# Adjacency counts in turns of sixteen parts, with one-hots of eight parts written side by side

## The reference

```python
# layer 0: mean over incoming edges
messages = h[src] @ W + b
out = segment_sum(messages, dst, N) / clip(deg, 1, None)[:, None]
# layer 3: h = relu(x @ W_in.T + b_in), then three times
out = segment_sum(norm * (h @ W.T)[row], col, N) + b
h = h + relu(out)
```

## Time and profile before

| | |
|---|---|
| median of 3 runs | 9669.24 us |
| profiled execution | 9702.59 us, span 9700.8 us |
| counting stage in it | 883 to 1957 us |
| TensorE, VectorE, ScalarE busy, whole span | 6251.8 (64%), 4831.9 (50%), 1756.7 us (18%) |
| mean granted clock of TensorE | 0.685 of 2.4 GHz |

### The profile page before, as it was taken

How to read it: one execution, slowest core, us unless ns; L and a number is a source line. 1 busy time by engine, 2 the same in 40 slices (tenths; PEclk the granted TensorE clock), 3 DMA queues, 4 the chain that set the end, 5 groups by cost and what they waited for, 6 DMA issues and landing times. The chain is left out here.

```text
span 9700.8 us, 148103 instructions
## 1 busy us (share of the span) xinstructions
PE 6251.8 (64%) x29798; PEld 4311.0 (44%) x29800; DVE 4831.9 (50%) x20045; ACT 1756.7 (18%) x3492; POOL 3219.5 (33%) x3353
## 2 busy tenths in 40 slices
PE   1512666677555455554555548777888888769999
PEld 1511333366333333333333325555555555568777
DVE  6887999932555555555555543333333333342222
ACT  0002666600111111111111111111111111110000
POOL 0103000000544444444444425555555555500000
PEclk9955555589666666666666665666666665669999
DMA  1051222254322222222222312222222222226666
GB/s 34 1 180 44 74 75 75 75 191 183 64 59 58 58 60 58 58 58 58 59 57 58 59 28 34 34 35 34 34 35 34 34 34 34 34 75 261 245 242 236
DMA packets 1052830, 765.90 MB, mean 79 GB/s; under 512 B 869013, under 2 KB 978277, under 8 KB 1033206
## 3 DMA queue, kind: packets, MB, share of 16 engines
q1 hardware_dynamic: 897158, 511.13, 18.3%
q0 software_dynamic: 131808, 243.11, 10.7%
q10 hardware_dynamic: 23776, 10.58, 0.4%
HBM read 659.36 MB, written 143.22 MB: 83 GB/s over the span
## 5 line engine op out<-in xcount | busy, mean ns | idle before, releaser
L1745 POOL DMA_INDIRECT rows<-node_rows_wide,idx_ring x1612 | 1533.9, 952 | 1649.4 <-DMA idx_ring<-sorted_pairs 1167.5
L1745 POOL DMA_INDIRECT rows<-node_rows,idx_ring x1612 | 1524.7, 946 | 1232.9 <-DMA idx_ring<-src_all 697.0
L1794 PE MATMUL ps_sum<-hots,act_ring 128*97 128x128 f32 x3224 | 742.1, 403 | 1536.5 <-DVE hots L1779 1184.2
L1794 PEld LDWEIGHTS ps_sum<-hots,act_ring 128*97 128x97 f32 x3224 | 612.6, 255 | 1908.2 <-DVE accT L1788 1448.8
L1782 DVE TENSOR_SCALAR hots<-iota,lane_all 128x128 f32<-128x128 f32 x1612 | 461.7, 287 | 1838.8 <-remote 1324.1
L1794 PE MATMUL ps_sum<-hots,msg 128*96 128x128 f32 x3224 | 724.2, 399 | 472.9 <-DVE hots L1782 239.2
L1821 PE MATMUL ps_e<-w1e,aT 128*128 128x384 f32 x1612 | 983.6, 757 | 25.1 <-DVE aT L1856 20.2
L1321 PE MATMUL ps_conv<-conv_rows,adj_ring 128*128 128x288 bf16 x7497 | 939.0, 287 | 47.3 <-DMA adj_ring<-adjacency 24.8
L1099 PE MATMUL ps_blocks<-dst_hot,src_hot 128*128 128x256 bf16 x2792 | 659.5, 416 | 410.6 <-ACT ps_blocks L1120 287.9
L1788 DVE TENSOR_TENSOR accT<-accT,ps_sum 97x128 f32 (+1 forms) x3224 | 907.1, 281 | 5.4 <-PE ps_sum L1794 4.0
L1794 PEld LDWEIGHTS ps_sum<-hots,msg 128*96 128x96 f32 x3224 | 624.9, 258 | 503.3 <-DVE accT L1788 411.7
(11 more groups left out here) (323 smaller groups left out, 6544.8 us busy)
## 6 DMA issues: line engine op xcount, KB each, us to landing
adj_ring<-adjacency SPq DMA_DIRECT2D x144, 2176.0 KB, 7.8
adjacency<-panels SPq DMA_DIRECT2D x588, 128.0 KB, 1.7
idx_ring<-sorted_pairs SPq DMA_DIRECT2D x1612, 1.0 KB
attr_ring<-sorted_attr SPq DMA_DIRECT2D x1612, 16.0 KB
rows<-node_rows_wide,idx_ring POOLq DMA_INDIRECT x1612
attr_ring<-sorted_attr SPq DMA_DIRECT2D x1612, 8.5 KB
rows<-node_rows,idx_ring POOLq DMA_INDIRECT x1612
sorted_attr<-in_edge_attr SPq DMA_DIRECT2D x5, 5000.0 KB
```

The lines of the kernel that those rows point to most:

```text
L1745: g.indirect_dma_start(out=rows[:, r, j, 0:width], out_offset=None, in_=table, in_offset=bass.IndirectOffsetOnAxis(ap=idx, axis=0)).then_i ...
L1794: last = pe.matmul(ps_sum[0:M, r % 2, j, :], what(r, j), hots[:, r % 2, j, :], start=True, stop=True)
```

## The change

- `GK` is 16, `HB` 2 and `BANKS` 8: a turn has sixteen parts, two turns are buffered, all eight banks are used, in plain rotation over all 637 panels. There are 175 turns, 2800 parts. The table entry of a part becomes its panel's number plus 1, and the bank is that number modulo 8.
- VectorE waits for the banks. For each half turn of eight parts (`HK`) it reads the table entry of the half's last part, waits for the matmuls that used the buffer, and waits on `emptied`. TensorE no longer reads or waits for that; it does one column load of 16 values a turn.
- The one-hots of eight parts come from one instruction each: `iota_h` now repeats each number eight times, the lanes of eight parts are read as a row of eight that repeats, and a TENSOR_TENSOR compare writes 128 x 8 and 256 x 8 values. Element (column, part) stands at 8 x column + part. So the matmul's operands, `src_hot[:, r, j // HK, :, j % HK]` and the same of `dst_hot`, have a step of eight bf16, 16 bytes, from column to column.
- ScalarE reads a block's 13 panel ends in one load, and its loop over blocks is written out for eight blocks, as the bank of a panel now depends on the block. A semaphore `passed_a` is counted up beside its wait.

```diff
--- before.py
+++ after.py
@@ -75,16 +75,17 @@
 BUCKETS = NB * NW
 NB_BITS = 64
 BASE = 0x20000000
-GK = 8
+GK = 16
+HALF = GK // 2
 LOG_P = 7
 PARTS = E // P + BUCKETS
 Q2 = -(-PARTS // GK)
 T2 = Q2 * GK
-HB = 4
+HB = 2
+HK = 8
 NK = -(-NW // 2)
 PANELS = NB * NK
-PANEL_BANK = tuple(k if k < 7 else k - 7 for k in range(NK))
-BANKS = 7
+BANKS = 8
 TT = -(-(T2 + 64) // P) * P
 KC = -(-T2 // (4 * P)) * 4
 TP = KC * P
@@ -97,7 +98,7 @@
 CB = SB // NC
 PANEL_COLS = tuple(min(2 * WD, NP - 2 * k * WD) for k in range(NK))
 assert CB * NC == SB and PANEL_COLS[NK - 1] == P
-assert TP <= 2 * SN and NK <= 13 and KEYS > E + P and NW <= 1 << WB and COLS % OCN == 0
+assert (NB - 1) % BANKS == 0 and TP <= 2 * SN and NK <= 13 and KEYS > E + P and NW <= 1 << WB and COLS % OCN == 0
 ZR = 8
 
 GB = 7
@@ -262,6 +263,7 @@
         gather_go = sem("gather_go")
         passed_t = sem("passed_t")
         passed_v = sem("passed_v")
+        passed_a = sem("passed_a")
         gathered = [sem(f"gathered{k}") for k in range(GPI)]
         src_kept = sem("src_kept")
         fields = sem("fields")
@@ -667,7 +669,7 @@
             part_to = accT[0:1, 0:2 * T2].bitcast(I32).rearrange("p (c t) -> p c t", c=2)
             panel_end = accT[64:65, 0:PANELS].bitcast(I32)
             lanes = tmp("lanes", [P, 2, TP], BF16)
-            iota_h = tmp("iota_h", [P, WD], BF16)
+            iota_h = tmp("iota_h", [P, WD, HK], BF16)
 
             with ExitStack() as ctx:
                 def stmp(name, shape, dt=F32):
@@ -709,7 +711,7 @@
                 put_at = stmp("put_at", [NB, NW + 1], I32)
                 info = stmp("info", [NB, NW + 1, 3])
                 panel_i = stmp("panel_i", [NB, 2, NW], I32)
-                panel_f = stmp("panel_f", [NB, 2, NW])
+                panel_f = stmp("panel_f", [NB, 1, NW])
                 end_i = stmp("end_i", [NB, NK], I32)
                 ps_t = ctx.enter_context(nc.psum_tensor("ps_keys", [P, 4, 512], F32))
                 ps_c = ctx.enter_context(nc.psum_tensor("ps_counts", [P, 512], F32))
@@ -720,7 +722,7 @@
                 @block.gpsimd
                 def _(g):
                     g.iota(lane_no[:, :], [[0, 1]], base=0, channel_multiplier=1).then_inc(made.sem, 1)
-                    g.iota(iota_h[:, :], [[1, WD]], base=0, channel_multiplier=0,
+                    g.iota(iota_h[:, :, :], [[1, WD], [0, HK]], base=0, channel_multiplier=0,
                            allow_small_or_imprecise_dtypes=True).then_inc(made.sem, 1)
                     g.memset(ones2[:, :], 1.0).then_inc(made.sem, 1)
                     g.memset(before2[:, :], 1.0).then_inc(made.sem, 1)
@@ -823,7 +825,7 @@
                     v.tensor_copy(end_i[:, NW // 2:NK], til_end[:, NW - 1:NW]).then_inc(ends_out.sem, 1)
                     step(v, v.memset(info[:, NW, 0:1], 1.0))
                     step(v, v.memset(info[:, NW, 1:2], float(NB << WB)))
-                    step(v, v.memset(info[:, NW, 2:3], float((PANELS + 2) << 12)))
+                    step(v, v.memset(info[:, NW, 2:3], float((PANELS + 1 << 12) + PANELS % BANKS * 2 * WD)))
                     link(v, v.tensor_scalar(row_no[:, 1:2], row_no[:, 0:1], float(1 << WB), None, ALU.mult))
                     step(v, v.tensor_scalar(info[:, 0:NW, 0], cnt[:, :], 1.0, None, ALU.add))
                     step(v, v.tensor_scalar(info[:, 0:NW, 1], iota[0:NB, 0:NW], row_no[:, 1:2], None, ALU.add))
@@ -838,18 +840,16 @@
                     of_window, panel = panel_i[:, 0, :], panel_i[:, 1, :]
                     link(v, v.tensor_copy(of_window, iota[0:NB, 0:NW]))
                     link(v, v.tensor_scalar(panel, of_window, 1, None, ALU.logical_shift_right))
-                    step(v, v.tensor_scalar(of_window, of_window, 1, 8, ALU.bitwise_and, ALU.logical_shift_left))
-                    link(v, v.tensor_copy(panel_f[:, 1, :], panel))
-                    step(v, v.tensor_copy(panel_f[:, 0, :], of_window))
-                    link(v, v.tensor_scalar(row_no[:, 1:2], row_no[:, 0:1], float(NK), 2.0, ALU.mult, ALU.add))
-                    link(v, v.tensor_scalar(til[:, :], panel_f[:, 1, :], row_no[:, 1:2], None, ALU.add))
-                    link(v, v.scalar_tensor_tensor(out=panel_f[:, 0, :], in0=panel_f[:, 1, :], scalar=512.0,
-                                                   in1=panel_f[:, 0, :], op0=ALU.mult, op1=ALU.add))
-                    link(v, v.tensor_scalar(panel_f[:, 1, :], panel_f[:, 1, :], float(BANKS), -512.0 * BANKS,
-                                            ALU.is_ge, ALU.mult))
-                    link(v, v.tensor_tensor(panel_f[:, 0, :], panel_f[:, 0, :], panel_f[:, 1, :], ALU.add))
-                    link(v, v.scalar_tensor_tensor(out=info[:, 0:NW, 2], in0=til[:, :], scalar=4096.0,
-                                                   in1=panel_f[:, 0, :], op0=ALU.mult, op1=ALU.add))
+                    step(v, v.tensor_scalar(of_window, of_window, 1, LOG_P + 1, ALU.bitwise_and, ALU.logical_shift_left))
+                    link(v, v.tensor_copy(til[:, :], panel))
+                    link(v, v.tensor_scalar(row_no[:, 1:2], row_no[:, 0:1], float(NK), None, ALU.mult))
+                    link(v, v.tensor_scalar(til[:, :], til[:, :], row_no[:, 1:2], None, ALU.add))
+                    link(v, v.tensor_copy(panel, til[:, :]))
+                    link(v, v.tensor_scalar(panel, panel, BANKS - 1, LOG_P + 2, ALU.bitwise_and, ALU.logical_shift_left))
+                    link(v, v.tensor_tensor(panel, panel, of_window, ALU.bitwise_or))
+                    link(v, v.tensor_copy(panel_f[:, 0, :], panel))
+                    link(v, v.tensor_scalar(til[:, :], til[:, :], 1.0, 4096.0, ALU.add, ALU.mult))
+                    link(v, v.tensor_tensor(info[:, 0:NW, 2], til[:, :], panel_f[:, 0, :], ALU.add))
 
                 def describe_tiles(v):
 
@@ -1049,8 +1049,8 @@
             with ExitStack() as ctx:
                 def btmp(name, shape, dt=F32):
                     return sbuf(name, shape, dt, ctx)
-                src_hot = btmp("src_hot", [P, HB, GK, P], BF16)
-                dst_hot = btmp("dst_hot", [P, HB, GK, WD], BF16)
+                src_hot = btmp("src_hot", [P, HB, GK // HK, P, HK], BF16)
+                dst_hot = btmp("dst_hot", [P, HB, GK // HK, WD, HK], BF16)
                 panels = btmp("panels", [P, NK, 2 * WD], F16)
                 target = btmp("target", [P, 2 * WD])
                 heavy_cell = btmp("heavy_cell", [P, NK, HV, 2 * WD], F16)
@@ -1067,15 +1067,19 @@
                     v.memset(no_lanes[:, :], 0.0).then_inc(nothing.sem, 1)
 
                     def hots(q, turn, r):
-                        past(v, block_mm, (q - (HB - 1)) * GK)
-                        v.sem_inc(passed_v.sem, 1)
-                        for j in range(GK):
-                            v.tensor_scalar(src_hot[:, r, j, :], iota_h[:, 0:P], lanes[:, 0, dyn(q * GK + j, 1)], None,
-                                            ALU.is_equal)
-                            last = v.tensor_scalar(dst_hot[:, r, j, :], iota_h[:, :], lanes[:, 1, dyn(q * GK + j, 1)], None,
-                                                   ALU.is_equal)
-                            if j % 4 == 3:
-                                last.then_inc(ends_hot.sem, 1)
+
+                        for n in range(GK // HK):
+                            if n * HK % HALF == 0:
+                                empty = v.value_load(part_to[0:1, 1, dyn(q * GK + n * HK + HALF - 1, 1)], min_val=1,
+                                                     max_val=PANELS + 1)
+                                past(v, block_mm, (q - HB) * GK + n * HK + HALF)
+                                v.sem_inc(passed_v.sem, 1)
+                                v.wait_ge(emptied.sem, empty)
+                            lane = [lanes[:, k, dyn(q * GK + n * HK, HK)].unsqueeze(1) for k in range(2)]
+                            v.tensor_tensor(src_hot[:, r, n, :, :], iota_h[:, 0:P, :],
+                                            lane[0].to_broadcast([P, P, HK]), ALU.is_equal)
+                            v.tensor_tensor(dst_hot[:, r, n, :, :], iota_h[:, :, :],
+                                            lane[1].to_broadcast([P, WD, HK]), ALU.is_equal).then_inc(ends_hot.sem, 1)
                     turns(v, [(hots, 0)], Q2, HB)
 
                 @block.tensor
@@ -1087,16 +1091,14 @@
 
                     def count(q, turn, r):
 
-                        panels_out = pe.value_load(part_to[0:1, 1, dyn(q * GK + GK - 1, 1)], min_val=2, max_val=PANELS + 2)
-                        pe.wait_ge(emptied.sem, panels_out)
-                        pe.sem_inc(passed_t.sem, 1)
                         at = nc.values_load_multi_w_load_instructions(
                             part_to[0:1, 0, dyn(q * GK, GK)], [PE], min_val=0, max_val=BANKS * 2 * WD - WD,
                             skip_runtime_bounds_check_because="a window's columns in one of the banks")[1]
                         for j in range(GK):
```

(32 more changed lines are left out.)

## The result

The changed kernel takes 9874.91 us (median of four runs, 9841.46 to 9896.57), the kernel before 9670.60 (now four runs, 9649.83 to 9679.14): a ratio of 1.021, 95% interval 1.0181 to 1.0239. It is slower by 204 us; forecast were 200.

The account below looks back on a forecast made before the run. VectorE was taken to set the pace of the closed 1074 us counting stage. Afterwards TensorE's 1268 us of matmuls plus some 6 us make 1274, +200 us, so a median of 9869 us; eight-in-ten range 9330 to 10010.

Parts of the forecast that it names:

- The matmul's step: Counting stage, TensorE: operand columns 16 bytes apart cost 1.77 ns each, 453 ns a matmul, 1268 us for 2800.
- The bucket counts: Trace line with columns 196 bf16 apart: 95.9 ns per 49-column load and 25-column matmul, giving bounds 1.30 and 1.96 ns.
- VectorE's row at 12 bytes: VectorE reads 12 bytes apart: 3841 ns for 2792 elements, 1.32 ns each, taken as 1.76 ns a 16-byte stretch.
- The weight load: TensorE in the counting stage: loading 128 stepped weight columns takes 227 ns and stays beside the matmul.
- What VectorE waits for: Counting stage: banks are always free in time, VectorE's moved wait ends early, and TensorE releases VectorE, idle half the stage.
- TensorE's queue: Counting stage: one column load of sixteen values a turn, an estimated 0.93 us, hidden; 163 us if it were not.
- The free step: Counting stage: the operands' step costs nothing and three engines are level; stage 718 us, total 9315 to 9430; chance 0.2.
- hidden in both: ScalarE in the counting stage: one load of 13 ends a block replaces 13 loads of 278 ns, neither costing time.
- The clock's rival: Busy TensorE gets the upper clock; a stepped column costs two cycles, 213 ns a matmul, total some 9330; chance 0.07.
- VectorE at one element at a time: VectorE's one-hot compares take 1176 us while the step is free; +105 to +130 us, total 9775 to 9800; chance 0.04.
- a column above 1.96 ns: TensorE's stepped columns in the counting stage cost more than the upper bound; total above 10005 us; chance 0.04.
- the cheaper column: TensorE's stepped columns cost 1.30 to 1.50 ns; stage 940 to 1081 us, total 9535 to 9676; chance 0.1.

Follow-up runs that it names:

- preheat: The changed kernel with 80 matmuls of 512 zero columns put before the stepped matmuls; 8061.5 us, the kernel before 7829.3 on that chip.
- step4_ends: The changed kernel with one-hots of four parts at once (8-byte step) and ScalarE's panel ends read singly; 7499.2 us against 7829.3 before, ratio 0.9575.

## Why the prediction was right

- **The matmul's step.** Predicted 1.77 ns a column, 453 ns a matmul, 1268 us; measured 1.79, 458, 1283 us (1.77 and 453 with flat weights). That the size came out so closely is in part luck. The bucket counts gave its bounds by charging their time to the weight columns, which the runs don't bear out (next point); the middle of these bounds is 1.63. Their 1.84 ns took the fixed 208 ns of a matmul from rows at a clock of 0.50, while their own row has 1.00; preheat's zeros, 512 columns in 379 ns at 1.00, leave some 166 ns fixed. What found the size was VectorE's row at 12 bytes, once it was read per line of 16 bytes (1.76 ns) and not per element (1.32). 10 bytes confirm that reading on TensorE.
- **The weight load.** I let 128 columns cost 227 ns and be hidden. Hidden is right; the price is not: with stepped weights and flat moving columns a pair goes by in 116 ns. So the 95.9 ns of the bucket counts are not explained by what a step costs in 128-column loads; whether the 49-column load, the moving side or the issue sets them stays open.
- **VectorE.** Predicted 1.76 us a half turn, with two-byte elements at twice the rate of four-byte ones; the two instructions last 0.70 and 1.22 us, and where nothing holds them a half starts 1.74 us behind the last (1503.03 and 1504.77 in the timeline). The Trainium skill's 1224 ns for 2048 elements (VectorE: DVE Perf Modes, "The perf-mode tier table") is met by 1223.
- **What VectorE waits for.** I wrote that the bank is always free in time and TensorE's buffers release VectorE. It waits 563 us for banks and 75 for matmuls, and with ScalarE's single loads 593 and 45: the eight banks and not the buffers hold it back. It costs nothing here, for TensorE always has parts in hand.
- **TensorE's queue.** Sixteen values were put at 0.93 us; the load lasts 1.2, hidden as said.
- **The rivals.** The free step did not come, and its price was wrong besides: 718 us predicted for the stage, 881 measured with flat operands. The step that failed in it is that the one load of 13 ends a block is "hidden in both": it is hidden in the changed kernel only. With that load undone step4_ends has a stage of 728 us; flat operands with single loads were not run. The clock's rival is refuted by preheat and by the changed kernel's first 3 us: the step costs no fewer ns at 1.00. Its premise failed as well, for a TensorE busy without a break had 0.50 from 892 us on. VectorE at one element at a time and a column above 1.96 ns did not occur; nor did the cheaper column.
- **The sum.** +200 us against +204 in the medians and +213 in the stage. The other stages of the profiled execution were 36 us shorter than before's, which lies within the spread of such executions (the kernel before took 9646.8 to 9723.1 us in seven runs on one chip).

## What to carry to other kernels

Count the 16-byte lines that a matmul's moving operand touches, not its columns: a layout that makes the writer's instruction long and cheap is paid for by the reader at 1.79 ns a line, whatever clock TensorE has. A step of 8 bytes cost 230 ns a matmul, where neighbours cost 213 at the lower clock and 116 at the upper, and still let VectorE build four parts at once. And when a bound moves away, look again at what it covered: a register load that was free behind TensorE was 154 us in front of it.

## What the runs showed of the hardware

- The cost of a stepped moving operand is graded by lines (8, 10, 16, 20 bytes: 230, 287, 458, 462 ns for 256 columns) and a time: 458 ns with 1.00 to 0.50 granted.
- Stepped weights of 128 columns cost little: with 16 bytes between columns a pair went by in a median of 116 ns at the upper clock, as with flat ones, and 4 to 5 ns came on top beside a stepped moving operand (458 for 453, 234 for 230 ns).
- TensorE busy without a gap for 1286 us was granted 0.50 for all but the first 3 us or so, and behind the preheating it lost the upper clock 3 us into the stepped matmuls; with 8 bytes it got 0.72 to 0.90, with 10 bytes 0.50.
- A load of 13 values to ScalarE's registers took 3.05 us, of one 0.28; of 16 to TensorE's 1.2 us.
